# A third buffer for the lane one-hots, and a softmax whose maximum is subtracted by four exponentials

## The reference

```python
att = jnp.sum(att_in * a, axis=-1)
att = jnp.where(att > 0, att, 0.2 * att)
m = jnp.maximum(jax.ops.segment_max(att, tgt, num_segments=num_nodes), 0.0)
ex = jnp.exp(att - m[tgt])
denom = jax.ops.segment_sum(ex, tgt, num_segments=num_nodes) + (num_edges - deg)[:, None] * jnp.exp(-m)
w = ex / denom[tgt]
h_prime = jax.ops.segment_sum(w[:, :, None] * h_src, tgt, num_segments=num_nodes)
```

## Time and profile before

| | |
|---|---|
| time, median of 3 runs | 1711.01 us (1710.84 to 1711.35) |
| the profiled execution | 1709.79 us, of which span 1707.9 us |
| busy over the span | PE 82%, DVE 63%, ACT 40%, POOL 8% |
| attention, 1107 to 1708 us | PE 452.7, DVE 481.5, ACT 410.7 us busy of 601; mean granted clock of PE 0.83 |

### The profile page before, as it was taken

How to read it: one execution, slowest core, us unless ns; L and a number is a source line. 1 busy time by engine, 2 the same in 40 slices (tenths; PEclk the granted TensorE clock), 3 DMA queues, 4 the chain that set the end, 5 groups by cost and what they waited for, 6 DMA issues and landing times.

```text
span 1707.9 us, 50127 instructions
## 1 busy us (share of the span) xinstructions
PE 1405.4 (82%) x22245; PEld 1015.4 (59%) x22245; DVE 1076.5 (63%) x2066; ACT 679.0 (40%) x1575; POOL 140.4 (8%) x99
## 2 busy tenths in 40 slices
PE   4969889896399999999996888737888886788885
PEld 4968878786344454454456878635555554555554
DVE  5499999999300010001117888888888887888873
ACT  3245655654100000001120000057777776677775
POOL 1511111110000000000000000011111111011000
PEclk9999999988699999999998998858888887788888
DMA  5638777756689799879944777400000000000000
GB/s 196 228 87 233 191 224 202 210 126 147 167 289 355 262 327 335 277 257 347 359 171 171 278 293 272 143 12 12 12 13 12 12 12 7 12 12 12 25 3 23
DMA packets 190933, 270.14 MB, mean 158 GB/s; under 512 B 16538, under 2 KB 119447, under 8 KB 190582
## 3 DMA queue, kind: packets, MB, share of 16 engines
q1 hardware_dynamic: 186710, 256.32, 45.7%
q0 software_dynamic: 4000, 10.54, 2.0%
HBM read 217.69 MB, written 49.14 MB: 156 GB/s over the span
## 4 chain that ended last, share of the span: by engine, by line
PE 45%; DVE 32%; DMA 9%; issue 5%; ACT 4%; DVEq 4%; SPq 1%; ACTq 1%; POOL 0%; POOLq 0%
PE bank L673 23%; PE bank L739 8%; DVE Hw L1156 8%; PE bank L750 7%; DVE L L1146 6%; DVE Hx L1332 6%; DMA hib<-slp 5%; DVE Lq L1325 4%; PE bank L710 3%; DMA drow<-in_dst,rowi 2%; ACT Att L1002 1%; DVEq L1150 1%; DVE Hh L1148 1%; DVE hib L1193 1%; DVEq L1278 1%
## 5 line engine op out<-in xcount | busy, mean ns | idle before, releaser
L1002 ACT COPY Att<-bank 128x400 f32<-128x400 f32 x800 | 335.0, 539 | 166.9 <-PE bank L739 166.2
L739 PE MATMUL bank<-Hx,Lq 64*128 64x100 f16 x6400 | 241.2, 223 | 87.9 <-DVE Hx L1332 82.1
L739 PEld LDWEIGHTS bank<-Hx,Lq 64*128 64x128 f16 x6400 | 176.6, 102 | 174.9 <-DVE Hx L1332 89.2
L750 PE MATMUL bank<-Att,xa 128*32 128x128 f32 x5000 | 242.3, 306 | 38.1 <-ACT oT L1009 38.1
L600 PE MATMUL bank<-L,Hw 128*52 128x128 bf16 x4800 | 178.9, 234 | 54.5 <-DVE Hw L1156 52.8
L1332 DVE TENSOR_TENSOR Hx<-Hq,wdup 128x832 f16<-128x832 f16 x400 | 205.3, 586 | 3.7
L600 PEld LDWEIGHTS bank<-L,Hw 128*52 128x52 bf16 x4800 | 154.7, 113 | 64.2 <-DVE Hw L1156 58.0
L710 PE MATMUL bank<-Tp,lob 128*128 128x100 bf16 x2418 | 161.3, 216 | 30.9 <-DVE sel L1264 29.0
L1156 DVE TENSOR_TENSOR Hw<-Hh,dup 64x832 bf16<-64x832 bf16 x300 | 175.9, 586 | 7.5 <-PE bank L600 0.4
L882 ACT COPY rows<-bank 116x512 f32<-116x512 f32 x200 | 117.2, 588 | 150.6 <-PE bank L600 134.1
L710 PEld LDWEIGHTS bank<-Tp,lob 128*128 128x128 bf16 x2418 | 154.7, 103 | 36.2 <-DVE sel L1264 26.1
(11 more groups left out here) (169 smaller groups left out, 1382.2 us busy)
## 6 DMA issues: line engine op xcount, KB each, us to landing
pieces<-adj SPq DMA_DIRECT2D x90, 1280.0 KB, 9.9
adj<-rows SPq DMA_DIRECT2D x100, 416.0 KB
lob<-slp SPq DMA_DIRECT2D x26, 992.0 KB, 6.2
hib<-slp SPq DMA_DIRECT2D x26, 992.0 KB, 5.0
ea<-in_edge_attr SPq DMA_DIRECT2D x25, 992.0 KB, 8.4
pieces<-adj SPq DMA_DIRECT2D x15, 320.0 KB, 3.2
lh_d<-dup SPq DMA_DIRECT2D x25, 64.0 KB, 5.4
lhd<-lh_d SPq DMA_DIRECT2D x25, 64.0 KB, 1.8
```

The costliest lines, as they stand in the source:

```text
L739: m = pe.matmul(bank[i % 3 * 2 + d][:, v * H * NB:(v + 1) * H * NB].rearrange("p (h i) -> p h i", h=H), Lq[n % 2][rows, pp, :], Hx[n % 2][ ...
L750: m = pe.matmul(bank[7][h * HD:(h + 1) * HD, 0:P], xa[:, i, h * HD:(h + 1) * HD], Att[j % 2][:, h * NB + i, :], start=(i == 0), stop=(i == ...
L1002: m = act.copy(o[:, d, :, :], bank[i % 3 * 2 + d][:, 0:4 * H * NB].rearrange("p (q i) -> p i q", q=4))
```

## The change

`Lq` gets a third buffer. Its wait for PE is therefore for one half earlier, and the old wait moves down to stand ahead of `Hx`. The waits of the first half of a block for `lhd` and `wdup` stay where they are.

In the softmax DVE no longer subtracts the maximum from the logits: it writes the masked logits to `am2`, and the negated maximum (4 columns) to `low`. ACT subtracts: `exps(j)` does one Exp for each head, of 64 columns, with a column of `low` as its bias, and each of them also gives the sum of its row in `esum`. DVE's sum of `ex` falls away.

```diff
-            Lq = [sb(f"Lq{i}", [P, HP, P], F16, c) for i in range(2)]
+            Lq = [sb(f"Lq{i}", [P, HP, P], F16, c) for i in range(3)]
...
-                                          Lq[n % 2][rows, pp, :], Hx[n % 2][rows, k, pp, :, 0:NB], start=(k == 0), stop=(k == 1))
+                                          Lq[n % 3][rows, pp, :], Hx[n % 2][rows, k, pp, :, 0:NB], start=(k == 0), stop=(k == 1))
...
-                act.activation(ex[:, j % 2, :, :], am2[:, j % 2, :, :], ACT.Exp)
+                for h in range(H):
+                    act.activation(ex[:, j % 2, h, :], am2[:, j % 2, h, :], ACT.Exp, bias=low[:, j % 2, h:h + 1],
+                                   accum_out=esum[:, j % 2, h:h + 1])
...
-                dve.tensor_reduce(mx[:, 0, :], am[:, 0, :, :], AX.X, ALU.max)
-                dve.drain()
-                dve.tensor_tensor(am2[:, v, :, :], am[:, 0, :, :],
-                                  mx[:, 0, :].rearrange("p (h o) -> p h o", o=1).broadcast_to([P, H, U]), ALU.subtract)
+                dve.tensor_reduce(mx[:, 0, :], am2[:, v, :, :], AX.X, ALU.max)
+                dve.drain()
+                dve.tensor_scalar(low[:, v, :], mx[:, 0, :], -1.0, None, ALU.mult)
...
-                dve.tensor_reduce(sm[:, 0, :], ex[:, v, :, :], AX.X, ALU.add)
...
-                dve.tensor_tensor(sm[:, 2, :], sm[:, 0, :], fe[:, v, 0, :], ALU.mult)
+                dve.tensor_tensor(sm[:, 2, :], esum[:, v, :], fe[:, v, 0, :], ALU.mult)
...
-                if n >= 2:
-                    dve.wait_ge(s["set_ps"], 8 * (n - 1))
-                dve.tensor_tensor(Lq[n % 2][:, :, :].rearrange("p u (n k) -> p u n k", k=2), pair_lo, spread(lhd[:, j % 3, 0, us, :], P // 2),
+                if n >= 3:
+                    dve.wait_ge(s["set_ps"], 8 * (n - 2))
+                dve.tensor_tensor(Lq[n % 3][:, :, :].rearrange("p u (n k) -> p u n k", k=2), pair_lo, spread(lhd[:, j % 3, 0, us, :], P // 2),
...
                 dve.drain()
+                if n >= 2:
+                    dve.wait_ge(s["set_ps"], 8 * (n - 1))
                 for k in range(2):
```

More of the change, by code:

```diff
@@ L169, in build @@
             zr = sb("zr", [P, 3, U, H], F32, c)
-            am = sb("am", [P, 2, H, U], F32, c)
+            am = sb("am", [P, 1, H, U], F32, c)
             am2, ex = sb("am2", [P, 2, H, U], F32, c), sb("ex", [P, 2, H, U], F32, c)
+            low, esum = sb("low", [P, 2, H], F32, c), sb("esum", [P, 2, H], F32, c)
             Z16 = sb("Z16", [P, 2, 2, H, P], F16, c)
@@ L1278, in logits_of @@
                 dve.drain()
-                dve.scalar_tensor_tensor(out=am[:, 1, :, :], in0=am[:, 0, :, :], scalar=0.2, in1=am[:, 0, :, :], op0=ALU.mult, op1=ALU.max)
+                dve.scalar_tensor_tensor(out=am[:, 0, :, :], in0=am[:, 0, :, :], scalar=0.2, in1=am[:, 0, :, :], op0=ALU.mult, op1=ALU.max)
                 dve.drain()
-                dve.scalar_tensor_tensor(out=am[:, 0, :, :], in0=negb[:, j, :].rearrange("p (o u) -> p o u", o=1).broadcast_to([P, H, U]),
-                                         scalar=GONE, in1=am[:, 1, :, :], op0=ALU.mult, op1=ALU.add)
+                dve.scalar_tensor_tensor(out=am2[:, v, :, :], in0=negb[:, j, :].rearrange("p (o u) -> p o u", o=1).broadcast_to([P, H, U]),
+                                         scalar=GONE, in1=am[:, 0, :, :], op0=ALU.mult, op1=ALU.add)
                 dve.drain()
-                dve.tensor_reduce(mx[:, 0, :], am[:, 0, :, :], AX.X, ALU.max)
+                dve.tensor_reduce(mx[:, 0, :], am2[:, v, :, :], AX.X, ALU.max)
                 dve.drain()
-                dve.tensor_tensor(am2[:, v, :, :], am[:, 0, :, :],
-                                  mx[:, 0, :].rearrange("p (h o) -> p h o", o=1).broadcast_to([P, H, U]), ALU.subtract)
+                dve.tensor_scalar(low[:, v, :], mx[:, 0, :], -1.0, None, ALU.mult)
                 dve.tensor_scalar(mx[:, 1, :], mx[:, 0, :], 0.0, None, ALU.max)
```

## The result

The changed kernel takes 1729.8 us (median of 4 runs, 1727.18 to 1731.75), against 1711.18 us (median of 4) for the kernel before on the same chip. The ratio is 1.0101, with an interval from 1.0077 to 1.0125: 1.0% slower. The forecast was 1728.5 us. The profiled execution took 1728.25 us, of which span 1726.4 us, so 18.5 us more span than before. Granted clock over the span is 0.916, before 0.907, so the extra time is not a lower clock. Beside the later experiments the kernel before ran 13 times, and one of these runs took 4274.89 us; the ratios leave it out.

The account below looks back on a forecast made before the run. Bound: a loop through `wdup`, DVE's `Lq` to `Hx`, PE's sets, ACT's exponentials and copies. Twenty blocks 18.4 us, block 1 0.3, less 1.2 saved on DVE: +17.5 on 1711.0, so 1728.5 us; range 1719 to 1747.

Parts of the forecast that it names:

- The wait that was misread: DVE's 49.2 us ahead of `Lq`, 22 waits labelled PE: predicted to be waits for `wdup`, which ends 0.09 us earlier.
- DVE's savings at nothing: Some 0.4 us off the logits and 0.4 off `weights_of`, outside the loop; counted in three places only, 1.2 us.
- The price of a pair: On ACT, one Exp of 64 columns plus the read of its row sum: 0.34 us, four 1.36.
- E: ACT's extra time per block for four Exp and read pairs instead of one Exp: 1.36 - 0.33 = 1.03 us.
- The term that no row showed: On ACT, a row-sum read without a drain behind it: 0.19 - 0.09 = 0.10 us, assuming overlap.
- The sum: Blocks 2 to 13 and 15 to 22: eleven pay 1.03 us, nine pay 0.78, together 18.4 us.
- the allowance for the clock: 5 us to either side, since a new period shifts the pattern of PE's stretches at 1.2 GHz.
- E of 0.63: Lower end of ACT's extra time, if the sum's read hid wholly: the forecast's sum gives 9.7 us, 1721 us.
- The rival of 36 us: PE's clock falls behind the new stop at its eighth set: 1.8 us a block, 36 us more, 1765 us; chance 0.1.

Follow-up runs that it names:

- the moved wait: Changed kernel with DVE's wait for `wdup` moved from ahead of `Lq` to ahead of the first `Hx`: 1654.16 us, ratio 0.9662 to the kernel before.

## Why the prediction was right

- **The wait that was misread.** The prediction put the 49.2 us down to `wdup` and not to PE, from 0.09 us between two rows. The third buffer alone (no change) and the moved wait (3.4%) show it from both sides.
- **The third buffer and DVE's savings at nothing.** Both hold. `Lq`'s 22 waits are 1.37 us longer in the mean (79.3 - 49.2 over 22); 0.83 of it is the longer period of the blocks ahead of them and 0.54 is what DVE saved. The prediction had sized that saving at 0.8: it gave no time to the operation of 4 columns that replaces the subtraction, and `low` takes 0.17 us. From a block's first `Lq` to its second DVE now takes 9.74 us where it took 10.00. The wait ahead of `Hx` has no row in the table of the changed kernel.
- **The price of a pair.** 0.335 us against 0.34, and E = 1.34 - 0.33 = 1.01 us against 1.03. The term that no row showed, a read of the sum without a drain behind it at 0.10 us, came from the overlap between neighbours. The run without the sums bears it out: the four reads add 0.37 us, 0.09 each.
- **The sum.** 18.7 us in twenty blocks, 18.4 predicted, and its split holds: the exponentials cost 20.4 us (20.6 predicted), and the waits for PE that ACT had behind them in nine blocks are gone, 2.4 us (2.25 predicted). The part with PE's stretch at 1.2 GHz is 0.7 us longer, which was in the allowance for the clock and not in the sum. On the other side block 1, block 14 and the two last blocks with the tail came out 1.7 us lower than predicted, which no run took apart. (For E of 0.63 the sum gives 9.5 us and not 9.7; nothing hangs on it.)
- **Luck in the last microsecond.** 1729.8 against 1728.5 us is closer than the method can claim. The attention grew by 16.3 us and not 17.5, the code ahead of it happened to be 2.1 us later in that execution, and the four runs of the changed kernel differ by 4.6 us among themselves.
- **The clock.** The rival of 36 us fell: behind the eighth set's stops of twenty blocks the granted clock is 1.00. The Trainium skill's rule of a PE that swings between its levels as it cycles through PSUM banks (TensorE: Matmul & The Clock Gate, section "A second HAM failure mode: psum-queue depth-cycling") is not borne out by the one stop there. Two close stops are the case that looks like it: those of block 14, and those at set 0 of every block, for `Hx` and for `oT`, with 0.53 behind them in the block shown above.
- **What I did not see.** I read that `Lq` stands behind `wdup`, and did not ask whether it needs to. It was worth 47 us to the kernel before (1712.8 to 1666.0, with its softmax and a third buffer) and 76 us to the changed one (1729.8 to 1654.2), more than the change cost by far.

Not tried: exponentials at another place in ACT's order, which needs another order on DVE too.

## What to carry to other kernels

- Where an instruction waits for several semaphores, hold its start against the end of each candidate; a constant lag of 0.1 us in every block names the true one, whatever the profile's label says.
- Find the loop that sets the pace and price an edit only by what it adds between the points where the loop passes over its engine: 1.1 us of the same work cost 16 us or nothing.
- The sign of an edit belongs to the bound: moving work from DVE to ACT cost 16 us while the loop ran over ACT, and gained 12 us once one needless wait was gone and DVE was the bound.

## What the runs showed of the hardware

The read of a row sum on ACT takes 0.19 us but adds only 0.09 (four of them 0.37, the changed kernel against the one without the sums), since it overlaps what stands on both sides. And a single stop of PE of 0.53 to 1.10 us at the eighth set, with PE busy behind it, left the granted clock at 1.00 in all twenty blocks of the changed kernel. In the kernel with the moved wait two close stops at set 0, of 0.46 to 1.71 us and of 1.30, were followed by 0.50 in ten blocks of eleven, and the one for `oT` alone, of 1.30 or 1.58 us, in one of nine.
